# Constant products at three slot heads, and a batch's preparation that the last batch leaves out, in a two-layer transformer kernel

## The reference

```python
h = _layernorm(x) * (1 + ca) + sa                   # ca, sa, ga, ...: from silu(c) @ wmod
x = x + ga * _L0_attn_ref(h, Wq, Wk, Wv)            # Q = h Wq^T, K, V; rotate; softmax(QK^T/sqrt(d)) V
h = _layernorm(x) * (1 + cb) + sb
x = x + gb * _L0_ffn_ref(h, w_gate, w_up, w_down)   # fp4(x) @ fp4(w).T; silu(gate) * up; fp4 again; down
h = _layernorm(x) * (1 + ca) + sa                   # layer 1's own ca, sa, ga, ...
x = x + ga * _L1_attn_ref(h, qk, ov)                # softmax(h qk h^T / sqrt(d)) h ov
h = _layernorm(x) * (1 + cb) + sb
# 8 experts, the best 2 by sigmoid(h gate_w^T + lb_bias); out += where(sel_e, y_e * wmean_e, 0); + shared
x = x + gb * _L1_ffn_ref(h, gate_w, lb_bias, ...)
```

## Time and profile before

| | us |
|---|---|
| median of 3 runs | 732.89 |
| lowest, highest | 732.48, 734.04 |
| the profiled execution's own time | 728.4 |
| its span, from the first to the last instruction | 726.6 |
| TensorE busy in the span | 639.8 (88%) |
| VectorE busy | 483.8 (67%) |
| ScalarE busy | 344.4 (47%) |
| GpSimd busy | 227.7 (31%) |
| mean granted clock of TensorE | 0.966 |

### The profile page before, as it was taken

One profiled execution on the slowest core, in us unless ns is written; L12 is line 12 of the kernel. 1 busy time (PEld: TensorE's weight loads), 2 busy tenths in 40 slices (PEclk: granted clock), 3 DMA queues, 4 the chain that ended last, 5 costly groups with the idle time before them and its releaser, 6 DMA issues.

```text
span 726.6 us, 10981 instructions
## 1 busy us (share of the span) xinstructions
PE 639.8 (88%) x3828; PEld 498.5 (69%) x3828; DVE 483.8 (67%) x1295; ACT 344.4 (47%) x708; POOL 227.7 (31%) x249
## 2 busy tenths in 40 slices
PE   5878899998788989988889999877889997899996
PEld 4356687877566778765677777756768784676774
DVE  5966598685777547637559685688556836766665
ACT  1144454555535464533445464444555453454553
POOL 3334555452644311005547254474310102000000
PEclk9999999999889999999999999969999999899999
DMA  8400000000000000000000000000000000001001
GB/s 270 107 1 1 1 2 1 1 1 1 1 0 1 1 1 1 1 2 1 1 0 1 1 1 1 1 1 1 1 1 1 1 1 1 1 14 30 14 24 35
DMA packets 12077, 9.63 MB, mean 13 GB/s; under 512 B 1708, under 2 KB 10744, under 8 KB 12024
## 3 DMA queue, kind: packets, MB, share of 16 engines
q1 hardware_dynamic: 12024, 8.94, 4.2%
HBM read 6.84 MB, written 2.10 MB: 12 GB/s over the span
## 4 chain that ended last, share of the span: by engine, by line
PE 69%; DVE 13%; ACT 8%; POOL 6%; issue 4%; DMA 1%; SPq 0%; ACTq 0%; POOLq 0%; DVEq 0%
PE ps L783 15%; PE ps L653 12%; PE ps L761 9%; PE ps L612 4%; PE ps L928 4%; PE ps L930 4%; PE ps L929 4%; PE ps L806 2%; PE ps L671 2%; PE ps L807 2%; PE ps L822 2%; ACT xn L1045 2%; PE ps L607 1%; PE ps L601 1%; PE ps L834 1%
## 5 line engine op out<-in xcount | busy, mean ns | idle before, releaser
L1105 ACT ACTIVATE probsT<-ps 128x512 f32<-128x512 f32 (+3 forms) x160 | 85.3, 533 | 171.3 <-PE ps L761 171.3
L783 PE MATMUL ps<-v_sb,probsT 128*128 128x129 f32 (+1 forms) x1148 | 158.1, 281 | 3.7 <-ACT probsT L1107 3.7
L783 PEld LDWEIGHTS ps<-v_sb,probsT 128*128 128x128 f32 (+1 forms) x1148 | 142.4, 192 | 10.9 <-ACT probsT L1107 5.5
L1374 DVE TENSOR_REDUCE row_max<-ps 128x1 f32<-128x512 f32 (+2 forms) x144 | 88.1, 620 | 57.9 <-PE ps L653 24.1
L761 PE MATMUL ps<-ident,probs 128*128 128x128 f32 (+1 forms) x574 | 93.9, 281 | 14.0 <-ACT hT L1035 7.1
L1079 ACT ACTIVATE probs<-ps,neg_max 128x512 f32<-128x512 f32 (+7 forms) x158 | 92.8, 618 | 12.4 <-DVE neg_max L1381 12.0
L761 PEld LDWEIGHTS ps<-ident,probs 128*128 128x128 f32 (+1 forms) x574 | 65.8, 140 | 45.5 <-issue 42.0
L511 POOL TENSOR_TENSOR hq<-ha,hp 128x352 f32<-128x352 f32 x32 | 29.9, 936 | 130.7 <-DVE hp L1417 130.7
L653 PE MATMUL ps<-k_high,q_high 128*128 128x512 f32 (+4 forms) x112 | 44.9, 401 | 3.4 <-ACT probs L1079 2.2
L1178 ACT ACTIVATE probs<-ps 128x512 f32<-128x512 f32 x40 | 24.0, 599 | 45.9 <-PE ps L930 45.9
L1609 DVE TENSOR_TENSOR probs<-probs,ps 128x512 f32<-128x512 f32 x40 | 27.4, 686 | 21.1 <-ACT probs L1178 20.5
(11 more groups left out here) (243 smaller groups left out, 1393.9 us busy)
## 6 DMA issues: line engine op xcount, KB each, us to landing
out<-x_sb SPq DMA_DIRECT2D x8, 256.0 KB, 2.3
x_sb<-in_L_attn_x SPq DMA_DIRECT2D x2, 512.0 KB, 5.9
hT_all<-in_L_wmod SPq DMA_DIRECT2D x2, 384.0 KB
rope_cos<-table_cos SPq DMA_DIRECT2D x1, 768.0 KB, 6.9
rope_sin<-table_sin SPq DMA_DIRECT2D x1, 768.0 KB, 8.1
rope_cos<-table_cos SPq DMA_DIRECT2D x1, 256.0 KB, 4.5
rope_sin<-table_sin SPq DMA_DIRECT2D x1, 256.0 KB, 6.0
moe_raw<-in_L_ffn_expert_gate_w SPq DMA_DIRECT2D x1, 256.0 KB, 3.9
```

The lines of the kernel that those rows point to most:

```text
L783: mm = pe.matmul(bank(OUT_AT, 0, V_W), probsT[0:size, n % 4, k * P:(k + 1) * P], v_sb[0:size, j, :], start=(c == 0 and k == 0), stop=(c == ...
L1105: ins = act.activation(probsT[:, n % 4, 0:full], bank(TURN, 0, full), ACT.Copy)
L1374: ins = dve.tensor_reduce(dst, ps[:, start:start + width], AX.X, ALU.max, negate=single)
```

## The change

- `WAITS_AT_HEAD` names three slots and a number of products: 11 in slot 6, 8 in slot 17, 10 in slot 21. In these slots `keep_clock(3, n)` stands ahead of the head's transposes, in both batches. Bank 3 holds scores only for tiles with more than 1536 keys.
- What prepares the next batch is issued only if there is one (`if b + 1 < BATCH`), on all engines.
- The counts of the semaphores for transposes are taken over both batches (`TURN_AT[b, *key]`), since the batches no longer have the same number; VectorE's steps are simply counted on.
- GpSimd's `scale_and_shift` waits for its own shift of the call before.

```diff
+WAITS_AT_HEAD = {FFN_LAG: 11, TILES + 1: 8, TILES + 5: 10}
...
-def input_turns(slot):
+def input_turns(batch, slot):
...
-    if slot == NEXT_SLOT:
+    if slot == NEXT_SLOT and batch + 1 < BATCH:
         turns.append(("next", 0))
...
-TURN_AT = {key: n + 1 for n, key in enumerate(turn_order())}
-IN_TURN = len(TURN_AT)
+TURN_AT = {key: n + 1 for n, key in enumerate([(b, *key) for b in range(BATCH) for key in turn_order(b)])}
+ALL_TURNS = len(TURN_AT)
...
                 pool.wait_ge(var_ready[0], n)
+                if n > 1:
+                    pool.wait_ge(shift_ready, n - 1)
...
-                    if s in (NEXT_SLOT - 2, NEXT_SLOT):
+                    if b + 1 < BATCH and s in (NEXT_SLOT - 2, NEXT_SLOT):
                         first_rsqrt((b + 1) * GROUPS + (s == NEXT_SLOT) + 1)
...
-                    if s == NEXT_SLOT:
+                    if b + 1 < BATCH and s == NEXT_SLOT:
                         out_of_bank(("next", 0))
...
-                    if s == NEXT_SLOT + 1:
+                    if b + 1 < BATCH and s == NEXT_SLOT + 1:
                         pe.wait_ge(roped, (b + 1) * 4 * GROUPS + 2)
                         project_0(0, 1)
...
-                    for key in input_turns(s):
+                    if s in WAITS_AT_HEAD:
+                        keep_clock(3, WAITS_AT_HEAD[s])
+                    for key in input_turns(b, s):
                         turn_group(key)
...
                 pe.wait_ge(logits_sum, b * GROUPS + GROUPS - 1)
-                first_values_and_scores(b, b * -1 + (BATCH - 1))
+                if b + 1 < BATCH:
+                    first_values_and_scores(b, b + 1)
                 keep_clock(GATE, 9)
...
-                put_v_at(0, (b + 1) * 2 * GROUPS)
+                if b + 1 < BATCH:
+                    put_v_at(0, (b + 1) * 2 * GROUPS)
                 copy_group(("norm3", GROUPS - 1))
-                first_exp(b)
+                if b + 1 < BATCH:
+                    first_exp(b)
...
-                    if s in (NEXT_SLOT, NEXT_SLOT + 1):
+                    if b + 1 < BATCH and s in (NEXT_SLOT, NEXT_SLOT + 1):
                         first_rotate(b, s - NEXT_SLOT, link)
...
-                first_maximum(b)
+                if b + 1 < BATCH:
+                    first_maximum(b)
                 take_logits(GROUPS - 1)
```

More of the change, by code:

```diff
@@ L128, in ffn_tile, with turn_order @@
     return slot - lag if 0 <= slot - lag < TILES else None
-def turn_order():
+def turn_order(batch):
     order = []
     for s in range(SLOTS):
-        order += input_turns(s)
+        order += input_turns(batch, s)
         for c in range(len(turn_chunks(*divmod(s, TILES)))):
@@ L156 @@
 parts_before, MAX_PARTS = before(lambda l, i: len(score_chunks(l, i)) if len(score_chunks(l, i)) > 1 else 0)
-STEPS_PER_BATCH = 177
 def build(nc, x, cos, sin, wq, wk, wv, w_gate, w_up, w_down, c0, wmod0, qk, ov, gate_w, lb_bias,
@@ L509, in hq_scaled @@
                     if n >= 2:
-                        pool.wait_ge(turned, b * IN_TURN + TURN_AT["hq", n - 2] + 1)
+                        pool.wait_ge(turned, TURN_AT[b, "hq", n - 2] + 1)
                     pool.tensor_tensor(hq[:, n % 2, :], ha[:], hp[:], ALU.add).then_inc(hq_step, 1)
@@ L521, in xq_scaled @@
                     if g >= 1:
-                        pool.wait_ge(turned, b * IN_TURN + TURN_AT["fp4_in", g - 1] + 1)
+                        pool.wait_ge(turned, TURN_AT[b, "fp4_in", g - 1] + 1)
                     pool.tensor_tensor(xq[:], qa[:], qp[:], ALU.add).then_inc(xq_step, 1)
@@ L545, in keys_low @@
                     cols = slice(g * BANK, (g + 1) * BANK)
-                    pool.wait_ge(copied, b * IN_TURN + TURN_AT["norm2", g] + 1)
+                    pool.wait_ge(copied, TURN_AT[b, "norm2", g] + 1)
                     pool.tensor_tensor(h_parts[1][:, cols], hT[:, cols], h_parts[0][:, cols].bitcast(F32),
@@ L687, in bank_free @@
                 def bank_free(key):
-                    pe.wait_ge(copied, b * IN_TURN + TURN_AT[key])
+                    pe.wait_ge(copied, TURN_AT[b, *key])
                 def out_of_bank(key):
-                    pe.wait_ge(copied, b * IN_TURN + TURN_AT[key] + 1)
+                    pe.wait_ge(copied, TURN_AT[b, *key] + 1)
                 def turn_group(key):
@@ L844, in logits @@
                         pe.wait_ge(gu_used, b * TILES + TILES)
-                    if g >= GROUPS - 2:
+                    if b + 1 < BATCH and g >= GROUPS - 2:
                         pe.wait_ge(roped, (b + 1) * 4 * GROUPS + 4)
@@ L882, in _ @@
                 pe.wait_ge(logits_sum, b * GROUPS + GROUPS - 1)
-                first_values_and_scores(b, b * -1 + (BATCH - 1))
+                if b + 1 < BATCH:
+                    first_values_and_scores(b, b + 1)
                 keep_clock(GATE, 9)
                 turn_group(("norm3", GROUPS - 1))
-                pe.wait_ge(v_ready, (b + 1) * 2 * GROUPS + 1)
+                if b + 1 < BATCH:
+                    pe.wait_ge(v_ready, (b + 1) * 2 * GROUPS + 1)
                 logits(GROUPS - 1)
@@ L891, in _ @@
             pe.wait_ge(logits_sum, BATCH * GROUPS)
-            pe.wait_ge(copied, BATCH * IN_TURN + 1)
+            pe.wait_ge(copied, ALL_TURNS + 1)
             for n in range(3 * UNITS):
@@ L1017, in filled @@
                 def filled(key):
-                    act.wait_ge(turned, b * IN_TURN + TURN_AT[key] + 1)
+                    act.wait_ge(turned, TURN_AT[b, *key] + 1)
                 def copy_group(key):
@@ L1076, in exp @@
                             last = len(turn_chunks(*divmod(s - 2, TILES))) - 1
-                            act.wait_ge(turned, b * IN_TURN + TURN_AT["probs", s - 2, last] + 1)
+                            act.wait_ge(turned, TURN_AT[b, "probs", s - 2, last] + 1)
                     width = min(width, SEQ - start)
@@ L1148, in _ @@
                         normalise_2(group_at(s, NORM2_SLOT + 1))
-                put_v_at(0, (b + 1) * 2 * GROUPS)
+                if b + 1 < BATCH:
+                    put_v_at(0, (b + 1) * 2 * GROUPS)
                 copy_group(("norm3", GROUPS - 1))
-                first_exp(b)
-                act.wait_ge(copied, b * IN_TURN + IN_TURN + 1)
+                if b + 1 < BATCH:
+                    first_exp(b)
+                act.wait_ge(copied, TURN_AT[b, "norm3", GROUPS - 1] + 1)
             act.wait_ge(logits_sum, BATCH * GROUPS)
@@ L1315, in _ @@
             first_maximum(-1)
-            setup_steps = steps[0]
             for b in range(BATCH):
[L1319 to L1324, removed]
                 def x_tile(t, n=1):
@@ L1451, in take_logits @@
                 def take_logits(g):
-                    dve.wait_ge(copied, b * IN_TURN + TURN_AT["norm3", g] + 1)
+                    dve.wait_ge(copied, TURN_AT[b, "norm3", g] + 1)
                     dve.tensor_copy(hT_all[:, bass.ds(b * SEQ + g * BANK, BANK)], hT_group[:])
@@ L1487, in _ @@
                     normalise_in_slot(s)
-                    if s in (NEXT_SLOT - 1, NEXT_SLOT + 1):
+                    if b + 1 < BATCH and s in (NEXT_SLOT - 1, NEXT_SLOT + 1):
                         first_normalise(b, BATCH - 1 - b, int(s > NEXT_SLOT))
```

## The result

| | median of runs, us | range | runs |
|---|---|---|---|
| before, beside it | 733.46 | 732.48 to 734.3 | 4 |
| after | 725.92 | 725.52 to 727.06 | 4 |

The ratio is 0.9906 (95% interval 0.9888 to 0.9924): 6.9 us faster by it, 7.5 us by the medians. The forecast was 726.2 us. The profiled execution of after has a span of 723.9 us.

The account below looks back on a forecast made before the run. TensorE, busy 88% of the span, was taken to pace the kernel, with some waits and half-speed stretches left. -2.9 - 4.2 + 0.5 = -6.6 us against 728.4 gave 721.8, scaled by 1.0062 to 726.2 us; range 720.5 to 730.5.

Parts of the forecast that it names:

- the fills: Heads of slots 6, 17 and 21: products inside TensorE's waits keep its clock up, 1.45 us gained a batch, 2.9 for two.
- the tail: Behind the second batch's slot 31: TensorE's wait grows from 0.59 to 2.2 us, the clock may fall; 0.5 us lost.
- Scaling by 1.0062: Step from the profiled execution to the runs' median: 732.89 us is 1.0062 times 728.4, so 721.8 becomes 726.2 us.
- Slot 6: Its head and gate product: kept clock gains 0.35 us a batch, as ScalarE is next in line; bounds 0 and 1.65.
- Slots 17 and 18: Longest slow stretch: 0 us, as the clock falls in a 3.8 us wait at slot 18 instead; bounds 2.27 and -1.
- Rival 2: The clock holds through slot 18: 2.27 us more a batch, 721.6 us; chance 0.13.
- Slot 21: Transposes, gate and up products at full clock take 1.78 instead of 2.85 us: 1.1 us gained a batch.
- The removal: Second batch's slots 28 and 29 lose the third batch's preparation: 2.51 and 1.72 us of TensorE work, 4.2 us gained.
- 1 (all half-speed time on the path): Half of 20.25 us a batch is saved, 20.2 us for both, and 4.2: 708 us; chance 0.03.
- 3 (only the removal pays): Later waits take back the gain of the fills: -4.2 + 0.5, 729.2 us; chance 0.20.
- 4: Second batch's tail: low clock also slows 15 transposes and 17 fills, 3.6 us late, 729.9 us; chance 0.07.
- 5: Fills meet a low clock and overrun, 6.3 us late a batch: slower, +8.4, 741 us; chance 0.04.

Follow-up runs that it names:

- before again: The kernel before, unchanged, run and profiled once more beside the experiments: 732.88 us, ratio 0.9988; its profile has a span of 731.5 us.
- e3: The changed kernel without the fill of slot 17, those of slots 6 and 21 kept: 727.6 us, ratio to before 0.9911.
- e1: The kernel before with only the fills of slots 6, 17 and 21 added, the third batch's preparation kept: 731.06 us, ratio to before 0.9980.
- e1b: Second run of the kernel before with only the fills of slots 6, 17 and 21 added: 731.24 us, ratio to before 0.9985.
- e4: The changed kernel with 16 more products at the head of slot 18: 717.7 us, ratio to before 0.9806.
- e6: The kernel of e4 with 4 and 6 products added at two waits in the setup: 720.14 us, ratio to before 0.9826.
- e10: The kernel of e4 with 11 and 17 instead of 9 products behind slot 31 and 3 before the last group's logits: 717.92 us, ratio to before 0.9807.
- e2: The changed kernel without its fills, so only the third batch's preparation removed: 727.07 us, ratio to before 0.9931.
- e7b: Second run of the changed kernel with doubled fills (22, 16 and 20 products): 726.36 us, ratio to before 0.9906.
- e5: The kernel of e4 with 16 instead of 9 products behind the second batch's slot 31: 718.75 us, ratio to before 0.9815.
- e7_double_fills: First run of the changed kernel with doubled fills (22, 16 and 20 products): 727.73 us, ratio to before 0.9931.

## Why the prediction was right, and where its terms were not

**The total** was right to 0.3 us, and its range held it. That it came so close is luck in part: the fills were priced too high and the tail had the wrong sign, and these two nearly cancel. The step from the profile to the median covered the rest: the sum said 721.8 us for a profiled execution, and after's took 725.7. Its span is only 2.7 us below that of the first profile, not 6.6, and 7.6 us below that of before again. Against the first profile it lost 2.0 us up to slot 6, 1.5 at the second batch's start and 1.3 in slot 25, all through stretches at 0.50. Scaling by 1.0062 (4.5 us) treated the first profile as a typical execution, only somewhat fast. It was one with fewer slow stretches.

**Slot 6**: forecast 0.35 us a batch. Against the first profile slots 6 to 17 are 0.52 and 0.55 us shorter; against before again 0.01, since the clock had not fallen there. The removal's trace, also without fills, shows both: 109.17 us in the first batch, where it fell, and 108.66 in the second, where it did not. So the fall costs 0.5 us where it comes, in 3 of these 6 batches. The term was the price of an event that not every execution has; it was priced as if each had.

**Slots 17 and 18**: forecast 0, the wait moving to slot 18 with 3.8 us and the fall with it. Measured: 3.84 us, clock 0.52 behind it, 17 to 18 unchanged. By its trace, e3 confirms that this fill is worth nothing as long as slot 18 has none. The stretch reaches to 209.4 instead of 206.25, so that slots 18 to 21 take 0.67 and 0.44 us more than in the first profile, within the -1 us kept as bound, and nothing against before again. Rival 2 fell.

**Slot 21**: forecast 1.1 us. Measured 1.06 and 1.06 against the first profile, 1.40 and 1.44 against before again. Its mechanism shows in the timeline of after the earlier trace rows:

```profile
230.12 0.63 PE L765 MATMUL ps<-ident,probs 128*128 128x128 f32 x4 [0.83 <-ACT hT L1043]
231.18 0.75 PE L811 MATMUL ps<-w_guT,xqT 128*128 128x352 f32 x2
```

From the transposes to the end of the up products it is 1.81 us; it was 2.85, and the forecast had 1.78.

So the fills' 2.9 us became some 1.1 to 1.5 in the timed runs. The interval of e1 reaches to 3.1 us, that of e1b to 2.6. Slot 6 is part of what is missing, but slot 21 alone gives 2.8 us against before again. The traces show something that the prediction's sum left out: a fall in slot 25, behind waits of 1.07 and 1.03 us. The same transposes in after and in the first profile of before:

```profile
543.57 1.01 PE L765 MATMUL ps<-ident,probs 128*128 128x128 f32 x4 [1.03 <-ACT hT L1043]
```

```profile
542.24 0.63 PE L761 MATMUL ps<-ident,probs 128*128 128x128 f32 x4 [1.03 <-ACT hT L1035]
```

It makes slots 25 to 30 1.2 to 1.4 us longer and comes in one batch of 6 of the 8 ordinary traces that have the fill of slot 21 and none at slot 25 (after, e1b, e3, e4, e6, e10), and in none of the 3 traces without fills. With so few traces, that the fill of slot 21 causes it is not shown; 2.8 less 1.3 us would fit the timed runs.

**The removal**: forecast 2.51 + 1.72 = 4.2 us; slots 28 and 29 are 2.59 and 1.72 us shorter, e2's stretch 4.31. TensorE was next in line throughout, as said. (In after, slots 25 to 30 are only 2.96 us shorter, since that fall in slot 25 lies in them.)

**The tail** failed in its sign: +0.5 us forecast, -1.08 and -1.32 measured, -1.27 in e2. The step "the wait grows to 2.2 us" was right, and the clock fell behind it, but after the logits, and at no cost. The prediction looked at the next 10 us only; nearly all of the 1.1 to 1.3 us comes 15 us later, from a stretch at 0.50 in the last stage. It is 6.8 us long in all three traces with the preparation (both of before, the fills alone) and 3.4 in eight of nine without it; in e7b, without it, it is 6.8 us again and the last part takes 123.07. So it goes with the removal in most executions, but nothing here shows what ties it to it: that stays open.

**Rivals.** 1 (all half-speed time on the path): slots 17 to 18 fall by 0.02 us where it wanted 4.5, so it fell. 3 (only the removal pays): slot 21 keeps its gain, but the fills' small total is near this rival, and the fall in slot 25 is of its kind. 4: the fall came, its work is hidden. 5: nothing started low, and e7b shows that even full doubling costs 1.6 us a batch, not 6.3 (29 more products of 0.233 us are 6.8): the waits behind a head, which ScalarE (before line 810) and GpSimd (at slot 18) end, absorb the rest.

The Trainium skill (TensorE: Matmul & The Clock Gate, Terms) prices half-rate time by throttled time times one minus the ratio of the clocks. From before again to after, 61.4 - 37.5 = 23.9 us at 0.50 are gone; by that rule that is 12.0 us, an estimate. The time outside the 4.3 us of removed work fell by 3.3 (7.6 - 4.3). The measurement decides: only slow work that the chain waits for comes back.

## What to carry to other kernels

Filling one wait of TensorE with constant products can just move the fall to the next wait, as at slot 17, where the fill gave nothing until slot 18 had one too: follow the chain of waits past the head, compute how long TensorE will then stand still, and fill that place as well. Before a clock stretch is priced from one profile, take a second one: stretches move between executions, the work that is removed does not. A fill may be generous when other engines end the waits behind it, since most of an overrun was given back here (4.7 of 6.3 us a batch).

## What the runs showed of the hardware

- Not only waits of 2 us and more are followed by falls, and not each of them is. After waits of 0.68, 0.87 and 0.33 us in a row (e5) the clock read 0.57 over 596.5 to 600.5 us; behind the 2.75 us at slot 6 it fell in 3 of 6 batches without fills. The setup had 6.7 us at 0.50 in before again and none in the first profile of the same code; after had 10.2.
- Two executions of kernels with fills took 1265.46 us (e1_fills_only) and 1081.5 us (e7_double_fills), both the first of their series, and none of the 74 of before beside the experiments took as long. In the latter the granted clock is 0.55 from 24 us to the end, neither of the two levels. In the former no window on TensorE shows a clock below 1.00, yet the 10 recorded fills of slot 6 take 4.94 us, and 2.32 in after: the granted clock of a profile doesn't show every slowing of TensorE. Why either happened is open, and whether the fills have a part in it.

```profile
24.00:1079.00 1055.00, 1018.35 (x3868) 0.55 0.01 3
```

```profile
121.83 4.94 PE L610 MATMUL ps<-unpick,ident_b 128*128 128x512 bf16 x10 [0.17 <-issue]
```
